# Selective-scan unit of 2048 columns multiplied in one GpSimd instruction instead of two, with a new order of the work

## The reference

```python
def step(h, inp):                       # selective scan, state 16 per channel, 256 channels
    u_t, d_t, b_t, c_t = inp
    dA = jnp.exp(d_t[:, :, None] * A)
    h = dA * h + (d_t * u_t)[:, :, None] * b_t[:, None, :]
    y = jnp.einsum('bdn,bn->bd', h, c_t)
    return (h, y)
...
xc = _silu(conv(xp)); dt, Bm, Cm = split(xc @ p['Wx']); delta = softplus(dt @ p['Wdt'] + p['bdt'])
y = (_selective_scan(xc, delta, A, Bm, Cm, p['Dp'])) * _silu(z);  return x + y @ p['Wblk']
...
topk_w, topk_idx = jax.lax.top_k(xt @ Ws + bs, 2)           # router, 8 experts
combine = jnp.sum(jax.nn.one_hot(topk_idx, 8) * softmax(topk_w)[..., None], axis=1)
out = sum over experts of combine * (silu(x @ Wg) * (x @ Wu)) @ Wd     # F = 344, all 8 computed
...
x = x + 0.5 * ffn(layernorm(x)); x = x + mamba4(layernorm(x)); x = x + 0.5 * ffn(layernorm(x))
```

## Time and profile before

| | |
|---|---|
| median of 3 runs | 4903.04 us (4896.58 to 4910.62) |
| the profiled execution's own time | 4894.95 us |
| its span on the core | 4893.2 us |
| busy, share of the span | POOL 88%, DVE 86%, PE 83%, ACT 71% |

### The profile page before, as it was taken

How to read it: one execution, slowest core, us unless ns; L and a number is a source line. 1 busy time by engine, 2 the same in 40 slices (tenths; PEclk the granted TensorE clock), 3 DMA queues, 4 the chain that set the end, 5 groups by cost and what they waited for, 6 DMA issues and landing times.

```text
span 4893.2 us, 50483 instructions
## 1 busy us (share of the span) xinstructions
PE 4054.7 (83%) x11584; PEld 1322.6 (27%) x11584; DVE 4230.6 (86%) x5503; ACT 3468.6 (71%) x5267; POOL 4288.1 (88%) x2281
## 2 busy tenths in 40 slices
PE   7767766888888888888888888888888888578869
PEld 2212222222222322232222222222222222122223
DVE  3558888999999999999999999999999999788853
ACT  4556776777777777777777777777777777667644
POOL 0469999999999999999999999999999999999960
PEclk9868787999999999999999999999999999788879
DMA  2233433343434334433443344334443434344210
GB/s 59 55 73 86 104 83 89 92 106 85 92 92 103 86 85 99 105 87 85 99 102 88 82 102 101 90 83 101 95 94 79 104 92 95 81 102 102 66 46 5
DMA packets 136626, 425.15 MB, mean 87 GB/s; under 512 B 15885, under 2 KB 35278, under 8 KB 135951
## 3 DMA queue, kind: packets, MB, share of 16 engines
q1 hardware_dynamic: 136335, 421.92, 36.9%
HBM read 145.04 MB, written 8.39 MB: 31 GB/s over the span
## 4 chain that ended last, share of the span: by engine, by line
POOL 27%; PE 25%; issue 17%; DVE 13%; ACT 7%; SPq 5%; DMA 5%; DVEq 0%; POOLq 0%; ACTq 0%
POOL work L814 15%; POOL work L804 9%; DVE work L624 6%; SPq L295 5%; DMA bc_sb<-bc_rows 5%; PE b_ps L365 4%; PE y_ps L337 3%; PE b_ps L353 3%; PE a_ps L359 3%; DVE s_ps L680 2%; PE a_ps L346 2%; POOL dd_src L823 2%; PE s_ps L425 2%; PE a_ps L353 1%; PE s_ps L435 1%
## 5 line engine op out<-in xcount | busy, mean ns | idle before, releaser
L814 POOL TENSOR_TENSOR work<-dd_sb,bc_sb 128x1024 f32<-128x1024 f32 x1024 | 2404.1, 2357 | 188.6 <-issue 77.6
L624 DVE TENSOR_TENSOR_SCAN work<-dA_ps,work 128x512 f32<-128x512 f32 x2048 | 2408.2, 1207 | 116.6 <-POOL work L814 62.1
L472 ACT ACTIVATE dA_ps<-dd_sb,a_sb 128x512 f32<-128x512 f32 x2048 | 1359.2, 682 | 676.3 <-DVE work L624 637.8
L804 POOL TENSOR_TENSOR work<-work,bc_sb 128x1024 f32<-128x1024 f32 x704 | 1659.6, 2358 | 6.8 <-DVE work L624 6.2
L337 PE MATMUL y_ps<-work,sel_sum 128*32 128x512 f32 x4096 | 619.6, 680 | 264.4 <-POOL work L804 221.9
L365 PE MATMUL b_ps<-sg_sb,wd_sb 128*128 128x512 f32 (+1 forms) x1536 | 734.1, 611 | 47.5 <-DVE sg_sb L714 47.5
L353 PE MATMUL b_ps<-xT_sb,wg_sb 128*128 128x512 f32 (+1 forms) x1024 | 616.4, 686 | 159.9 <-DVE acc_sb L699 95.3
L359 PE MATMUL a_ps<-xs_sb,wu_sb 128*128 128x512 f32 (+1 forms) x1024 | 563.8, 633 | 5.0 <-DVE sg_sb L714 3.3
L714 DVE TENSOR_TENSOR sg_sb<-sg_sb,a_ps 128x512 f32<-128x512 f32 (+1 forms) x512 | 343.9, 672 | 171.7 <-PE a_ps L359 171.4
L504 ACT ACTIVATE sg_sb<-b_ps 128x512 f32<-128x512 f32 (+1 forms) x512 | 303.5, 593 | 160.2 <-PE b_ps L353 151.7
L365 PEld LDWEIGHTS b_ps<-sg_sb,wd_sb 128*128 128x128 f32 (+1 forms) x1536 | 293.6, 195 | 438.6 <-issue 326.1
(11 more groups left out here) (99 smaller groups left out, 4169.1 us busy)
## 6 DMA issues: line engine op xcount, KB each, us to landing
dd_sb<-dd_src SPq DMA_DIRECT2D x512, 512.0 KB, 8.6
bc_sb<-bc_rows SPq DMA_DIRECT2D x256, 512.0 KB, 6.5
xr_sb<-in_L_attn_x SPq DMA_DIRECT2D x16, 256.0 KB, 2.9
bc_rows<-dbc_sb SPq DMA_DIRECT2D x128, 32.0 KB, 1.7
out<-xr_sb SPq DMA_DIRECT2D x16, 256.0 KB, 4.7
wg_sb<-in_L_ffn_Wg SPq DMA_DIRECT2D x1, 1376.0 KB
wu_sb<-in_L_ffn_Wu SPq DMA_DIRECT2D x1, 1376.0 KB
wd_sb<-in_L_ffn_Wd SPq DMA_DIRECT2D x2, 512.0 KB
```

The source lines that it names most:

```text
L472: act.activation(dA_ps[:, g % NDA, :], dd_sb[:, b, c, 0, :], ACT.Exp, scale=a_sb[:, l, b, j, c:c + 1]).then_inc(dA_ready, 1)
L624: dve.tensor_tensor_scan(tile, dA_ps[:, g % NDA, :], tile, 0.0, ALU.mult, ALU.add).then_inc(scanned, 1)
L804: pool.tensor_tensor(work[:, g % RING], work[:, g % RING], bc_sb[:, j, 0, :].unsqueeze(1).broadcast_to([128, 2, T]), ALU.mult).then_inc(po ...
L814: pool.tensor_tensor(work[:, g % RING], dd_sb[:, b, 2 * (i % 2):2 * (i % 2) + 2, 1, :], bc_sb[:, j, 1, :].unsqueeze(1).broadcast_to([128, ...
```

## The change

Step (1) becomes one instruction of 2048 columns for a unit. In step (4) POOL's product of the units 1, 4 and 7, in which DVE has no share, becomes one instruction of 2048 columns that waits for all four scans; in the other units POOL still multiplies the first half, after two scans, and DVE the second. The ring is counted in units, 3 of them, with the same size in memory. The router's comparison becomes eight instructions of one column each, with the expert's number as a scalar, where it was two of 32 columns. All tables of ticks have new numbers.

```diff
-RING, NDA = 6, 3
+RING, NDA = 3, 3
...
-CORE = {"exp": -12, "scan": 0, "dbu": -16, "dve_prod": 8, "pool_prod": 12, "c": -3, "sum": 24, "y0": 91, "y1": 18}
+CORE = {"exp": -11, "scan": -2, "dbu": -16, "dve_prod": 13, "c": 1, "sum": 22, "y0": 89, "y1": 11, "pool_prod": 6}
...
-        work = sb("work", [128, RING, 2, T])
+        work = sb("work", [128, RING, NG, T])
...
-                    dve.wait_ge(dbu_ready, g // 2 + 1)
+                    dve.wait_ge(dbu_ready, g // NG + 1)
...
-                        at_i = mf_sb[:, :, i].unsqueeze(2).broadcast_to([128, TB, E])
-                        last = dve.tensor_tensor(eq_sb[:, i], iota_e[:, :].unsqueeze(1).broadcast_to([128, TB, E]), at_i,
-                                                 ALU.is_equal)
+                        for k in range(TB):
+                            last = dve.tensor_scalar(eq_sb[:, i, k, :], iota_e[:, :], mf_sb[:, k, i:i + 1], None, ALU.is_equal)
...
-                if (at := part_at(t, CORE["pool_prod"], 8)) and not (at[2] % 2 == 1 and at[2] // 2 in DVE_UNITS):
-                    k, w, i = at
-                    j, g = (i // 2) % NJ, HALVES * k + i
-                    pool.wait_ge(scanned, 2 * g + 2)
+                if (at := part_at(t, CORE["pool_prod"] + 6, 16)) and at[2] not in DVE_UNITS:
+                    k, w, u = at
+                    g = UNITS * k + u
+                    pool.wait_ge(scanned, NG * g + NG)
                     pool.tensor_tensor(work[:, g % RING], work[:, g % RING],
-                                       bc_sb[:, j, 0, :].unsqueeze(1).broadcast_to([128, 2, T]), ALU.mult).then_inc(pool_prod, 1)
-                if at := part_at(t, CORE["dbu"], 8):
-                    k, w, i = at
-                    u, g = i // 2, HALVES * k + i
-                    b, j = u // NJ, u % NJ
+                                       bc_sb[:, u % NJ, 0, :].unsqueeze(1).broadcast_to([128, NG, T]), ALU.mult).then_inc(pool_prod, 1)
+                if (at := part_at(t, CORE["pool_prod"], 16)) and at[2] in DVE_UNITS:
+                    k, w, u = at
+                    g = UNITS * k + u
+                    pool.wait_ge(scanned, NG * g + 2)
+                    pool.tensor_tensor(work[:, g % RING, 0:2], work[:, g % RING, 0:2],
+                                       bc_sb[:, u % NJ, 0, :].unsqueeze(1).broadcast_to([128, 2, T]), ALU.mult).then_inc(pool_prod, 1)
+                if at := part_at(t, CORE["dbu"], 16):
+                    k, w, u = at
+                    g, b, j = UNITS * k + u, u // NJ, u % NJ
                     pool.wait_ge(dd_loaded[b], 64 * (k + 1))
                     pool.wait_ge(bc_loaded[j], 16 * (k + 1))
                     if g >= RING:
-                        pool.wait_ge(summed, (g - RING) // 2 + 1)
-                    pool.tensor_tensor(work[:, g % RING], dd_sb[:, b, 2 * (i % 2):2 * (i % 2) + 2, 1, :],
-                                       bc_sb[:, j, 1, :].unsqueeze(1).broadcast_to([128, 2, T]), ALU.mult).then_inc(dbu_ready, 1)
+                        pool.wait_ge(summed, g - RING + 1)
+                    pool.tensor_tensor(work[:, g % RING], dd_sb[:, b, :, 1, :],
+                                       bc_sb[:, j, 1, :].unsqueeze(1).broadcast_to([128, NG, T]), ALU.mult).then_inc(dbu_ready, 1)
```

More of the change, by code:

```diff
@@ L22 @@
 NJ, NG, SEL = 4, 4, 32
-UNITS, HALVES = NBLK * NJ, NBLK * NJ * 2
-RING, NDA = 6, 3
+UNITS = NBLK * NJ
+RING, NDA = 3, 3
 W, PERIOD = 128, 32
-CORE = {"exp": -12, "scan": 0, "dbu": -16, "dve_prod": 8, "pool_prod": 12, "c": -3, "sum": 24, "y0": 91, "y1": 18}
-PREP = {"sq": -30, "ms": 7, "rms": 6, "xn": 17, "xp0": 11, "conv0": 18, "xp1": 22, "conv1": 26, "silu_xc": 30, "z0": 30,
-        "zc0": 31, "z1": 39, "zc1": 33, "silu_z": 62, "wx": 40, "dbc": 42, "rows": 6, "dt0": 48, "sp0": 51, "delta0": 62,
-        "du0": 83, "dt1": 77, "sp1": 77, "delta1": 85, "du1": 116, "dd0": 38, "dd1": 115, "bc": 42}
@@ L35 @@
[L35 to L41, removed]
@@ L42 @@
-START = {"load": -130, "bn": -52, "nb": -50, "xtok": -50, "xt": -44, "xT": -49, "lg": -44, "lg_sb": -38, "mx": -33,
-         "mi": -27, "gap": -29, "we": -29, "eq": -22, "den": -28, "inv": -24, "comb": -23, "ct": -16, "gates": -21}
-END = {"yt": 17, "xo": 22, "bn": 22, "nb": 26, "xtok": 68, "ht": 79, "h": 74, "store": 76}
+CORE = {"exp": -11, "scan": -2, "dbu": -16, "dve_prod": 13, "c": 1, "sum": 22, "y0": 89, "y1": 11, "pool_prod": 6}
+PREP = {"sq": 2, "ms": 7, "rms": 8, "xn": 13, "xp0": 10, "conv0": 16, "xp1": 21, "conv1": 24, "silu_xc": 31, "z0": 29,
+        "zc0": 32, "z1": 35, "zc1": 34, "silu_z": 63, "wx": 39, "dbc": 45, "rows": 1, "dt0": 42, "sp0": 52, "delta0": 58,
+        "du0": 69, "dt1": 75, "sp1": 80, "delta1": 85, "du1": 94, "dd0": 46, "dd1": 97, "bc": 80}
@@ new lines @@
+NEAR = {"sq": 32, "ms": 37, "rms": 35, "xn": 45, "xp0": 41, "conv0": 48, "xp1": 53, "conv1": 56, "silu_xc": 63, "z0": 60,
+        "zc0": 67, "z1": 66, "zc1": 69, "silu_z": 95, "wx": 69, "dbc": 70, "rows": 75, "dt0": 74, "sp0": 82, "delta0": 87,
+        "du0": 85, "dt1": 84, "sp1": 92, "delta1": 93, "du1": 99, "dd0": 76, "dd1": 111, "bc": 75}
+POST = {"wblk": 84, "h": 89, "attn": 97, "x2": 106}
+POST_NEAR = {"wblk": 11, "h": 32, "attn": 32, "x2": 40}
+FFN_AT = {"gb": -1, "xs": 5, "g0": 1, "g1": 2, "g2": 4, "burst": 9, "u0": 5, "u1": 10, "u2": 18, "hh0": 16, "hh1": 18,
+          "hh2": 27, "down": 28, "acc": 36}
@@ L47, in phase_table @@
+START = {"load": -130, "bn": -68, "nb": -60, "xtok": -51, "xt": -46, "xT": -45, "lg": -43, "lg_sb": -37, "mx": -36,
+         "mi": -32, "gap": -38, "we": -28, "eq": -24, "den": -33, "inv": -23, "comb": -23, "ct": -17, "gates": -19}
+END = {"yt": 15, "xo": 20, "bn": 23, "nb": 47, "xtok": 70, "ht": 72, "h": 76, "store": -19}
 def phase_table():
@@ L121, in post_at, with dve_products @@
     return None
[L124 to L130, removed]
+def dve_products(k, u):
+    return k * NDP + sum(1 for v in DVE_UNITS if v <= u)
 def build(nc, x, norm_w, Win, conv_w, conv_b, Wx, Wdt, bdt, A_log, Dp, Wblk, Wout, bout,
```

43 lines of the change are left out of this document (21 added, 22 removed).

## The result

The changed kernel takes 4943.93 us (4941.66 to 4946.48, 5 runs), the kernel before 4896.62 us beside it: ratio 1.0092 with a 95% interval of 1.0074 to 1.0111. It is 47 us slower, where 4825 was forecast. The time is outside the range, and on the other side. The mean granted clock of the two profiled executions is the same, 0.915 before and 0.914 after, so it does not make the difference.

The account below looks back on a forecast made before the run. POOL was taken to set the pace, DVE close behind. Per phase -1.65 - 1.8 + 1.7 = -1.75 us, 112 us in all; DVE's share left 38 to 112, 80 taken: 4825 us, own range 4765 to 4865, 8-in-10 range 4765 to 4925.

Parts of the forecast that it names:

- the comparison: Router on DVE: eight instructions cost the pair's 0.5 to 1.2 us for each of 32 routers; uncovered, under 16 us.
- rival (c): Router's comparison is held by POOL's running long product, up to 3.5 us each, 112 us in all: 4925 us; chance 0.13.
- The merging: POOL's `dbu` and products of units 1, 4, 7: 0.15 us saved per merge, 1.65 a phase, 106 us in all.
- The wait at the phase's start: POOL at unit 0 of the next phase: its wait for `bc0` goes, saving 1.8 us a phase.
- The new one for `bc2`: POOL before unit 2's `dbu`: `bc2` comes late behind `dd1`, adding 1.7 us a phase, ends 0 and 5.9.
- The hand-over: POOL before whole products of units 1, 4, 7, now needing four scans: nothing added, ends 0 and 1.3 us.
- POOL's 112 us and DVE's 38: Whole-run gain: 112 us if POOL's saving counts fully, 38 if DVE's idle not caused by POOL stays; 80 taken.
- order: Phase start and unit 2: 1.8 us saved at `bc0` less 1.7 lost at `bc2`, 0.1 us a phase.
- Rival (d): POOL before whole products of units 1, 4, 7: hand-over too coarse, slower, about 4960 us; chance 0.12.
- its mark: Sign of too coarse a hand-over: POOL waits over 90 us for scans from 1000 to 4000 us.
- Rival (b): A merged POOL instruction costs as much as two, only the DMA term is left: 4897 to 4877 us; chance 0.04.
- (a): DVE is the bound and its waits stay: gain 6 us, time about 4897 us; chance 0.13.

Follow-up runs that it names:

- experiment 1: Changed kernel with the router's comparison done for the first feed-forward only, output not the reference's: 4841.58 us, 0.9881 of the kernel before.
- experiment 3: Changed kernel with the comparison moved from DVE to POOL, as a difference and a test for zero: 4841.3 us, ratio 0.9877 to the kernel before.
- experiment 4: Kernel before with its comparison left out for all but the first feed-forward: 4897.15 us, ratio 0.9993 to the unedited kernel before.
- experiment 2: Changed kernel with the old comparison, two instructions of 32 columns with two tensor inputs, in the same place: 4889.34 us, ratio 0.9974 to the kernel before.
- experiment 9: Kernel before with only its comparison changed to eight instructions of one column: 4924.96 us, ratio 1.0048 to the kernel before.
- experiment 6: Kernel before with comparison on POOL and the changed kernel's order (new tick tables), POOL instructions still in halves: 4898.13 us, ratio 0.9997 to the kernel before.
- experiment 12: Experiment 8's kernel with one tick number changed, so that SP starts `bc2` ahead of `dd1`: 4830.89 us, ratio 0.9861 to the kernel before.
- experiment 8: Changed kernel with comparison on POOL and the whole products of units 1, 4, 7 as two halves in place: 4833.44 us, ratio 0.987 to the kernel before.
- the table: Four kernels, comparison on POOL: old tick tables with halves 4916.42 us, with merged instructions 5299.93; new tables with halves 4898.13, with merged 4841.3.
- experiment 10: Changed kernel with one tick number changed, the comparison one scan later in DVE's order: 4887.86 us, ratio 0.9977 to the kernel before.
- experiment 11: Changed kernel with comparison on POOL and each `dbu` as two halves in place, reported ready after the second: 4882.32 us, ratio 0.997 to the kernel before.
- experiment 5: Kernel before with only the comparison moved to POOL, old tick tables and halves kept: 4916.42 us, ratio 1.0038 to the kernel before.

## Why the prediction was wrong

**The step that failed** is the comparison: "DVE's idle time hides the difference, and with that cover gone it is under 0.5 x 32 = 16 us". It was put at its old price, while the POOL instruction beside it went from 2.35 to 4.5 us and its two instructions became eight. Experiments 1, 3 and 4 show 102 us for the comparison in the changed kernel, none that can be measured in the kernel before. Of these the hold with the old pair is 48 us and the new form 55 (experiment 2). The hold stood in the text as rival (c), with its place, its 3.5 us and its row, and a chance of 0.13. Its place and its kind were right. That its price came near was luck in part: 112 us were forecast for the hold alone, and the 107.8 us of the line are 71 of hold (2.2 us for a router, not 3.5) and 37 of the eight instructions, which the rival did not count. The time of that rival, 4925, was 19 us low, and its base was 17 us low. The chance was wrong. It leaned on "the new one has one" SBUF input, for which there was no row either way. The runs show that the form makes no difference to the hold: the longest is 1.10 us with two inputs and 1.08 with one (experiment 9) beside products of 2.35 us, 3.94 with two (experiment 2) and 3.92 with one beside products of 4.5. The rule against that argument stood in the rival itself: the Trainium skill, Advanced Engine Details and Errata, section "VectorE Performance Modes", has `tensor_scalar` from SBUF to SBUF in the 2-port modes. The Trainium skill, SBUF — State Buffer, section "SBUF: two separate sides", has such an instruction and a GpSimd one exclude each other. By these the new form is held like the old one, and the trace agrees. No run here tells whether it is that mode or the scalar operand that makes the one-input form wait.

**The cost of the new form by itself** was missed. The "0.5 to 1.2 us" had been read from a pair that was held at times. Unheld, the pair takes 0.27 us and the eight, whose lengths overlap, 1.15: 28 us in 32 routers, not under 16. DVE's idle time does not hide it, since POOL waits behind it: 55 us in the changed kernel (experiment 2), 26 in the old one (experiment 9).

**The merging** was right in kind and nearly in size. Where POOL goes straight on from a 2048-column instruction to another long one, the starts are 4.45 to 4.51 us apart, at the median 4.49, against 4.47 forecast: 0.14 us saved for a merge where 0.15 was taken (1024 columns take 2.314 us at the median, by the same reading of the kernel before). The Trainium skill (GPSIMD Engine Reference, section 3.1) gives 4497 ns for an add of that size, and the trace agrees within 0.01 us. POOL's busy time fell by 96 us of 106. Its worth in time was lower: 57 us (experiments 6 and 3), which bears out that not all of POOL's gain is kept.

**The wait at the phase's start** went as forecast: `bc0` is in time. The new one for `bc2` is there, 1.04 us at 2022.41, but only in part of the phases: 19 us in the stretch, 0.5 for a phase where 1.7 was forecast. Experiment 12 shows that without the comparison on DVE it costs next to nothing.

**The hand-over** was put at nothing, with 1.3 us for a phase as an end. It is worth 8 us net of the split's own cost and some 23 at most (experiment 8), within the 83 that this end makes in 64 phases. Rival (d) is out: POOL waits 144 us where the prediction had set 90 us as its mark, but the mark was a bad one. Part of the 144 us followed from the comparison (experiment 1), and the 90 us left without it were mostly slack that other waits took up (experiment 8).

**Without the comparison** the forecast would have held: 4841.58 against 4825, within its own range of 4765 to 4865. The middle between POOL's 112 us and DVE's 38 was 80; the runs show 55 to 60 against the kernel before (4897 to 4842). So the rest of the sum held as a total, within its ends of 38 and 112; how it divides between merging and order (1.65 and 0.1 us for a phase) is less sure, for the table gives 57 us and 18. Rival (b) is out by the starts, (a) by experiments 1 and 3.

## What to carry to other kernels

When a POOL instruction is made longer, price every DVE instruction that a running one can hold by what is left of the longer instruction, not by its old length; move it to another engine or to where POOL's instruction is about to end (one tick number was worth 56 us here), and don't split it, since the first piece is held all the same. Judge a merging together with the order it stands in: the same one was worth -57 or +384 us. A wait is not a cost until a run without it is faster: 90 us of waits went in experiment 8 and 37 in experiment 12, and the time moved by 8 and 2.5.

## What the runs showed that was not expected

- A comparison of 8 columns with one tensor input and one scalar per partition is held by POOL as much as one with two tensor inputs: maximum 3.92 us beside a product of 4.5 us, 1.08 us beside one of 2.35.
- The reciprocal of 4 columns, also from SBUF to SBUF, was not held: in experiment 10, 27 of the 32 ran while a product ran on POOL, and none of these took over 0.16 us. The search for the best experts (`max` and its index) and the norm's statistics were not held either: 0.30 us at the longest in the changed kernel, most of them beside a long POOL instruction.
- A POOL instruction's fixed part of 0.14 us, 512 times, costs 41 us of time where 77 had been priced (experiment 11), although POOL was busy 96.0% of the stretch.
- Work of 27 us added to POOL cost nothing against leaving it out (experiments 3 and 1), where POOL was 95.3% and 94.7% busy, but 19 us in the kernel before (experiment 5), where it was 95.7% busy. The busy share alone does not tell the two cases apart.
